# A vision tower on one core: routing tables written earlier, a new order at the experts' start, a decay-attention head on VectorE, and grouped last stores

## The reference

```python
h = _L0_tok_ref(x, ...)                              # patches, class token, positions
h = _layernorm(h + _L0_attn_ref(h, ...))             # 16 heads of 16, causal
h = _layernorm(h + _L0_ffn_ref(h, ...))              # int8 fake-quantised MLP
h = _layernorm(h + _L1_attn_ref(h, ...))             # decay attention
h = _layernorm(h + _L1_ffn_ref(h, ...))              # fixed-point MLP
h = _layernorm(h + _L2_attn_ref(h, ...))
h = _layernorm(h + _L2_ffn_ref(h, ...))              # 8 experts, top 2
h = _layernorm(h + _L3_attn_ref(h, ...))             # latent attention with rope
h = _layernorm(h + _L3_ffn_ref(h, ...))              # fake-quantised gated MLP
```

## Time and profile before

| what | us |
|---|---|
| three runs | 1116.05, 1113.37, 1104.77 |
| median | 1113.37 |
| the profiled execution | 1114.32 |
| its span, first to last instruction | 1112.5 |
| share of the span: PE 82%, PEld 61%, DVE 55%, ACT 47%, POOL 30% | |
| mean granted TensorE clock | 0.888 |

### The profile page before, as it was taken

The page is one execution under the profiler, slowest core; times in us unless marked ns, Lnnn a source line. Parts: engine busy times, 40 slices in busy tenths (PEclk is TensorE's granted clock), DMA queues, the critical chain, the costliest instruction groups (busy, mean ns, idle before and its releaser), DMA issues. The chain is left out here.

```text
span 1112.5 us, 26159 instructions
## 1 busy us (share of the span) xinstructions
PE 909.6 (82%) x10336; PEld 674.0 (61%) x10336; DVE 606.8 (55%) x1306; ACT 527.1 (47%) x940; POOL 335.2 (30%) x426
## 2 busy tenths in 40 slices
PE   4889958389999789958996299999478998989564
PEld 4878735267777557647885144444267777777332
DVE  3566746656666469764664524232655573542585
ACT  2354638366656379735452155554123333442354
POOL 1203320545544100021323315442254553432101
PEclk8999958699999979879997599999799998989775
DMA  5300020200000000001001963222320000000001
GB/s 181 118 3 2 3 105 15 80 1 2 1 0 1 12 35 0 1 4 47 3 3 54 392 225 73 40 47 41 73 81 3 2 3 2 3 3 1 1 1 44
DMA packets 23973, 47.40 MB, mean 43 GB/s; under 512 B 4386, under 2 KB 15640, under 8 KB 23221
## 3 DMA queue, kind: packets, MB, share of 16 engines
q1 hardware_dynamic: 19524, 39.09, 10.1%
q0 software_dynamic: 4336, 6.74, 3.3%
HBM read 38.35 MB, written 7.47 MB: 41 GB/s over the span
## 5 line engine op out<-in xcount | busy, mean ns | idle before, releaser
L2731 PE MATMUL psum<-L2f_EW,weights_even 128*64 x176 | 83.0, 616 | 2.9 <-ACT weights_even L2430 2.1
L2732 PE MATMUL psum<-L2f_W,weights_even 128*64 128x512 f32 x176 | 83.0, 616 | 0.0
L2391 POOL DMA_INDIRECT expert_sums<-weights_even,L2f_target x20 | 36.5, 1825 | 77.8 <-DVE weights_even L2613 68.4
L2626 DVE TENSOR_TENSOR weights_even<-psum,weights_even 128x512 f32<-128x512 f32 x22 | 15.2, 692 | 77.1 <-PE psum L2732 75.1
L1057 PE MATMUL psum<-L_cT,weights_odd 128*128 128x222 f32 (+1 forms) x192 | 45.2, 366 | 12.7 <-DVE L_by_sin L944 11.0
L2438 ACT ACTIVATE L2f_W<-L2f_EW 128x1024 f32 x44 | 46.3, 1053 | 15.4 <-DMA L2f_EW<-experts 8.2
L2247 PE MATMUL psum<-weights_even,L1f_H 128*111 128x256 f32 x176 | 47.3, 427 | 7.4 <-DVE L1f_H L2178 7.4
L2731 PEld LDWEIGHTS psum<-L2f_EW,weights_even 128*64 128x64 f32 x176 | 22.9, 140 | 46.6 <-issue 46.6
L419 ACT ACTIVATE L_PT<-psum 101x296 f32<-101x296 f32 x64 | 27.0, 421 | 48.2 <-PE psum L615 48.1
L876 ACT ACTIVATE L_U<-psum 128x592 f32<-128x592 f32 x32 | 21.2, 663 | 60.0 <-PE psum L1108 60.0
L2247 PEld LDWEIGHTS psum<-weights_even,L1f_H 128*111 128x111 f32 x176 | 35.1, 202 | 18.7 <-DVE L1f_H L2178 8.7
(11 more groups left out here) (459 smaller groups left out, 2627.2 us busy)
## 6 DMA issues: line engine op xcount, KB each, us to landing
L2f_EW<-experts SPq DMA_DIRECT2D x24, 512.0 KB, 7.4
weights_even<-L_w SPq DMA_DIRECT2D x4, 1024.0 KB
patch_ring<-patches SPq DMA_DIRECT2D x11, 333.0 KB
expert_sums<-L_blank SPq DMA_DIRECT2D x1, 1184.0 KB
out<-X SPq DMA_DIRECT2D x10, 111.0 KB
weights_odd<-L_wo SPq DMA_DIRECT2D x1, 1024.0 KB
expert_rows<-X SPq DMA_DIRECT2D x1, 960.0 KB
expert_sums<-X SPq DMA_DIRECT2D x1, 960.0 KB
```

Of the source, the lines that this page charges most:

```text
L2731: nc.tensor.matmul(core.bank(bank)[PAIR[0], :], xsT[:, j % 2, c, PAIR[0]], own, start=c == 0, stop=c == KD - 1)
L2732: mm = nc.tensor.matmul(core.bank(bank)[PAIR[1], :], xsT[:, j % 2, c, PAIR[1]], cols(W1[:, part], KD, NF)[:, c], start=c == 0, stop=c == K ...
```

## The change

Four edits stand in the diff.

1. Tables: the copies of X into `expert_rows` and `expert_sums` move from the experts' stage into the pair attention of the stage before. As soon as a unit of two tiles is normalised (units 0 to 4, so tiles 0 to 9), SP starts four transfers for it: 96 and 15 rows into each table. Only the last tile's 74 rows are still copied in the experts' stage, before and behind the weights. The two semaphores live in `Route` now.
2. Experts' order: on VectorE `source_and_target()` runs ahead of the owners, and on ScalarE `x_T(0)` runs ahead of the up copy.
3. Decay head: the first tile's statistics run ahead of the wait for the stage's weights, its normalising runs on VectorE (three instructions, semaphores `rstd_of_first` and `x_first`) with only the reciprocal standard deviation left on GpSimd, and the low parts of the weights are cut into one in front of the loop and three behind the low part of the first transposed tile.
4. Last stage: the final norm runs in groups of 4, 4, 2 and 1 tiles, the first three on ScalarE; the stores go out by group, each as 96 and 15 rows (the last as 64 and 10); and the first gate step waits for four transposed blocks, the second for all six.

```diff
@@ pair_attention, sync
+                    for u in range(NU - 1):
+                        sp.wait_ge(norm_done, u + 1)
+                        for table, sem in (("expert_rows", route.rows_out), ("expert_sums", route.sums_out)):
+                            by_row = core.dram[table][2 * u * R:2 * (u + 1) * R, :].rearrange("(t p) d -> p t d", p=R)
+                            for rows in (slice(0, 96), slice(96, R)):
+                                sp.dma_start(by_row[rows], X[rows, 2 * u:2 * (u + 1), :]).then_inc(sem, 16)
                     sp.wait_ge(blank_out, 16)
@@ decay_attention, gpsimd
-                    if live(i, 0):
+                    if isinstance(i, int) and i == 0:
+                        pool.wait_ge(pvar, 1)
+                        rstd_on_pool(core, prs[:R, 0], pmv[:R, 0, 1:2]).then_inc(rstd_of_first, 1)
+                    elif live(i, 0):
@@ decay_attention, vector
+                input_stats(0, 0)
                 dve.wait_ge(mine[0], mine[1])
                 for j in range(4):
                     nc.vector.tensor_copy(mask[:R, j, :], w["mask_tri"])
+                dve.wait_ge(rstd_of_first, 1)
+                nc.vector.tensor_scalar(xin[:R, 0], X[:R, 0, :], pmv[:R, 0, 0:1], prs[:R, 0], ALU.subtract, ALU.mult)
+                dve.drain()
+                nc.vector.tensor_tensor(xin[:R, 0], xin[:R, 0], w["L1_gamma"], ALU.mult)
+                dve.drain()
+                nc.vector.tensor_tensor(xin[:R, 0], xin[:R, 0], w["L1_beta"], ALU.add).then_inc(x_first, 1)
+                low_part(0)
                 nc.vector.tensor_copy(decay[:R], w["decay"]).then_inc(set_up, 1)
...
-                    if isinstance(i, int) and i == 0:
-                        for n_, c in enumerate("akqv"):
-                            dve.wait_ge(w_high, n_ + 1)
-                            nc.vector.tensor_tensor(W[1][:, n_], cols(w[f"L1_w{c}"], KD, DI), W[0][:, n_], ALU.subtract).then_inc(w_low, 1)
+                    if isinstance(i, int) and i == 1:
+                        for n_ in range(1, 4):
+                            low_part(n_)
@@ decay_attention, tensor
-                        pe.wait_ge(x_staged, f + 1)
+                        if isinstance(f, int) and f == 0:
+                            pe.wait_ge(x_first, 1)
+                        else:
+                            pe.wait_ge(x_staged, f)
@@ experts_ffn, sync
-                for p in SPLIT:
-                    sp.dma_start(by_tile(rows, p, 0, WHOLE), X[p, 0:WHOLE, :]).then_inc(rows_out, 16)
-                sp.dma_start(rows[WHOLE * R:B * T, :], X[AGAIN:R, WHOLE, :]).then_inc(rows_out, 16)
+                sp.dma_start(rows[WHOLE * R:B * T, :], X[AGAIN:R, WHOLE, :]).then_inc(route.rows_out, 16)
@@ experts_ffn, scalar
                 second_half(0, GATE, gate_1)
+                x_T(0)
                 act.wait_ge(ups_in, 16 * NEX)
                 second_half(0, UP, up_1)
-                x_T(0)
@@ experts_ffn, vector
                 V.scalar_tensor_tensor(counts, first, 1.0 / 64.0, blocks, ALU.mult, ALU.add)
+                source_and_target()
                 dve.drain()
@@ quantised_glu
+        ENDS = [(0, 4), (4, 4), (8, 2), (10, 1)]
+        ON_ACT = 3
-        tail = SplitNorm(core, st, sb)
+        tail = SplitNorm(core, st, sb, ENDS)
...
-                for t in range(NT):
-                    ...
+                for t0, k in ENDS[:ON_ACT]:
+                    sp.wait_ge(tail.act_norm, t0 + k)
+                    by_row = out[t0 * R:(t0 + k) * R, :].rearrange("(t p) d -> p t d", p=R)
+                    for rows in (slice(0, 96), slice(96, R)):
+                        sp.dma_start(by_row[rows], X[rows, t0:t0 + k, :]).then_inc(stored, 16)
+                sp.wait_ge(tail.dve_norm, 1)
+                for rows in (slice(skip, skip + 64), slice(skip + 64, R)):
+                    sp.dma_start(out[(NT - 1) * R + rows.start - skip:(NT - 1) * R + rows.stop - skip, :], X[rows, NT - 1, :]).then_inc(stored, 16)
...
-                pe.wait_ge(xt_done, NXB)
                 for n, (g, c) in enumerate(steps):
+                    if n < 2:
+                        pe.wait_ge(xt_done, 4 if n == 0 else NXB)
```

More of the change, by code:

```diff
@@ L1340, in _, with input_stats, low_part @@
             def _(dve):
+                def input_stats(i, p):
+                    nc.vector.bn_stats(pstat[:R, p], X[:R, i, :])
+                    dve.drain()
+                    nc.vector.bn_aggr(pmv[:R, p], pstat[:R, p]).then_inc(pvar, 1)
+                def low_part(n):
+                    dve.wait_ge(w_high, n + 1)
+                    nc.vector.tensor_tensor(W[1][:, n], cols(w[f"L1_w{'akqv'[n]}"], KD, DI), W[0][:, n], ALU.subtract).then_inc(w_low, 1)
+                input_stats(0, 0)
                 dve.wait_ge(mine[0], mine[1])
@@ L1354, in scores_out @@
                                                   core.bank(u)[:R, 0:4 * R]).then_inc(s_done, 1)
-                    if live(i, 0):
-                        after(dve, x_staged, i - 1)
-                        nc.vector.bn_stats(pstat[:R, p], X[:R, i, :])
-                        dve.drain()
-                        nc.vector.bn_aggr(pmv[:R, p], pstat[:R, p]).then_inc(pvar, 1)
+                    if live(i, 0) and not (isinstance(i, int) and i == 0):
+                        after(dve, x_staged, i - 2)
+                        input_stats(i, p)
                     if F:
@@ L2544, in _, with source_and_target @@
                                         inside_b[:R, u, p].unsqueeze(2).broadcast_to([R, k, 128]), ALU.is_equal).then_inc(placed, 1)
+                def source_and_target():
+                    dve.wait_ge(mark_ps, 1)
+                    found = core.bank(4)[:, 0:2 * NS]
+                    V.tensor_scalar(empty[:], found[:, 0:NS], ROUND, ROUND + 1.0, ALU.add, ALU.subtract)
+                    dve.drain()
+                    V.tensor_tensor(mark[:], empty[:], found[:, NS:2 * NS], ALU.add)
+                    dve.drain()
+                    V.tensor_scalar(source[:], mark[:], 0.0, None, ALU.max).then_inc(source_done, 1)
+                    V.tensor_scalar(empty[:], mark[:], 0.0, w["spare_row"], ALU.is_lt, ALU.mult)
+                    dve.drain()
+                    V.scalar_tensor_tensor(target[:], mark[:], w["own_sums"], empty[:], ALU.add, ALU.add).then_inc(target_done, 1)
                 V.scalar_tensor_tensor(counts, first, 1.0 / 64.0, blocks, ALU.mult, ALU.add)
+                source_and_target()
                 dve.drain()
@@ L2916, in _ @@
                         finish(t - 3)
-                tail.on_dve(dve, 2)
+                tail.on_dve(dve, 3)
             @block.scalar
@@ L2956, in _ @@
                 tail.on_act(act, 1)
+                tail.on_act(act, 2)
             @block.tensor
```

47 lines of the change are left out of this document (14 added, 33 removed).

## The result

The changed kernel took 1092.6 us (median of four runs, 1088.4 to 1096.4) beside 1109.2 for the kernel before: 16.6 us less by the medians. The ratio is 0.9845, with a 95% interval of 0.9802 to 0.9888, which is 17.2 us. A second measurement of the same pair gave 0.984 (0.9781 to 0.9899). The forecast was 14.6 us less. It started from a median of 1113.37 for the kernel before; a fourth run brought that median to 1109.2. The profiled execution has a span of 1086.6 us, 25.9 less than before. That is more than the change gave, as the lengths of the stages show. Each is taken from the first instruction of a stage to that of the next.

What follows compares the result with a forecast made beforehand. Stage heads and tails were taken as chains of waits, the experts' tiles as TensorE-bound, the end as transfers. Terms 4.6 + 0 + 3.0 + 0.7 + 6.3 = 14.6 us off 1113.37 gave 1098.8; range 1088 to 1107.

Steps and rivals of the forecast that it cites:

- Decay head, 4.6 forecast: Start of the decay attention: first projection starts 4.6 us earlier, bounds 3.3 to 4.95.
- The 3.3: Decay head's low bound: mask copies could slow GpSimd as the weight split did, leaving a term of 3.3 us.
- Tables, 0: Table transfers moved into the pair attention: cost 0 there, at most 1 us.
- the prediction's sign: Experts' start: after the change VectorE does not wait for the down weights.
- Experts' order, 3.0: Experts' start: first gate matmul comes 3.0 us earlier, bounds 1.5 to 4.0.
- The 22 tiles behind start earlier by as much: Experts' tiles: all start earlier by the head's 3.0 us, since TensorE fills them.
- Last stage, 0.7 + 6.3: Last stage: first gate step 0.7 us earlier; end of the last stores 6.3 us earlier, bounds 5.0 and 6.8.
- term 6.8: Final stores: by the skill page the last 64 KB land 2.15 us behind their start, making the gain 6.8 us.
- (b): Stores: the row split fails and few engines serve them; only 8.3 us come, time 1105; chance 0.08.
- (a): Experts gain nothing: the gather or gate product takes up what the weights give free; time 1102; chance 0.15.
- (d): Experts' tiles or decay head: broken-up starts keep TensorE's clock at 1.2 GHz; four such tiles give 1117; chance 0.05.
- case (c): More comes: weights flowing alone shorten gather and half clock, or upper bounds throughout; about 1095 to 1091; chance 0.10.

Runs made afterwards that it cites:

- e2: Changed kernel with both table copies put back in the experts' stage, ahead of and behind the weights: experts' stage 199.6 us, ratio to the kernel before 0.9906.
- e6: Changed kernel with only the first tile's normalising put back on GpSimd: first projection at 8.0 us, decay stage 176.2 us, second pair attention 108.3 us.
- e7: Changed kernel with only ScalarE's order put back, up copy ahead of the first tile's evacuation: first gate matmul at 30.7 us, experts' stage 196.8 us.
- e4: Changed kernel with stores by group but not cut by rows: 12.6 us from last norm to the end, ratio to the kernel before 0.9948.
- b1: Kernel before, with only the last stage's first gate step waiting for four transposed blocks: its first gate matmul at 8.4 us, experts' stage 203.9 us.
- e5: Changed kernel with only the weights' low parts put back in one piece ahead of the loop: first projection at 9.3 us, decay stage 179.2 us.

## Why the prediction was right, step by step

**Decay head, 4.6 forecast; 5.4 at the projection, 6.0 and 4.0 over the stage.** The path was as told, but the gain at the projection lies above the term's upper bound of 4.95. The masks were mis-sized: I let them end 1.9 behind the stage's start, and they ended 1.2 behind it, since the statistics cost nothing there. That gave nothing by itself, for VectorE then waited 0.78 for GpSimd's result. The 0.8 us came in small pieces: that result 0.2 sooner than taken (1.96 behind the start for 2.15), VectorE's split, sums copy and statistics 2.05 in place of 2.4, and the low part and the step to the projection 0.4 in place of 0.6. GpSimd's deviation took 0.9 as taken. The 3.3 in which the mask copies slow GpSimd did not come: only the first of its two steps ran beside them, in 0.24, and it was VectorE that waited, for the memset.

**Tables, 0.** Right for the transfers, by e2, e6 and the starts. The transfers cost the attention nothing. What they removed was worth more than the prediction says: it has VectorE's wait for the downs as a step with no price. One reading was too quick: at 411 GB/s the downs were to be in 33 to 34 us behind the stage's start, and they landed at 37.0, with the DMA at 381 GB/s over the first 30 us. So VectorE did wait for them, against the prediction's sign, but for less time than TensorE had left. e2 is 4.8 and 2.8 us of stage longer than the two executions of the changed kernel, and the experts were 5.0 and 3.0 shorter than before.

**Experts' order, 3.0; 3.1 and 2.5 at the first gate matmul.** Each step stood: gather, then gate product, which came last of the two, then transpose, evacuation, number. In the first execution two sizes were off and cancelled, which is luck: the product ended 28.9 us behind the stage's start (28.3 forecast) and the number's load was overlapped to 0.24. In the second the load took 0.81. Beside the early tables only VectorE's move carries it, ScalarE's nothing (e7). Over the stage it came to 5.0 and 3.0. The 5.0 are the 3.1, 0.6 that the second tile no longer lost to the number's load (0.22 for 0.81), and by my estimate 1.3 of the clock (half of 2.5), which rose 3.0 us behind the first gate matmul and not 5.6; in the second execution it rose at 5.8. "The 22 tiles behind start earlier by as much" was therefore only a floor in that one.

**Last stage, 0.7 + 6.3.** The first gate step gained 0.9 and the last norm came 0.4 earlier relative to the last matmul (0.7 and 0.4 forecast). The last bytes landed 2.4 us behind the last norm's end (1085.7 against 1083.38) and not 3.0: from that norm to the span's end it is 6.7 us less. The estimate by the Trainium skill's page DMA: Bandwidth & Descriptors, section Anatomy of one DMA (2.15 behind the start, term 6.8), was the better one, with 2.2 measured; I had leaned on the scatter's 4.0. The page gives its figure for transfers that GpSimd starts, and these were SyncE's.

**Rivals.** (b) is dead by e4, (a) by the first gate matmul. (d) did not come in the tiles (clock 1.00 from 625.85 on), but a clock that falls at a pause is real: it costs about 3 us in b1's experts and 1.5 in e2's (the rest of e2's loss is the wait itself). In the pair attention the changed kernel runs 3.4 us at half the clock, by my estimate 1.7 of the 2.2 it lost there.

**The sum.** The range held (1088 to 1107). The median of 1092.6 lies 6.2 below the forecast of 1098.8, in case (c), and most of that is not a larger gain: 4.2 of it are the base, which came out at 1109.2 and not 1113.37. The other 2.0 to 2.6 us are the gain above the 14.6, and that is within what the ratio's interval leaves open (12.4 to 22.0 us). The prediction's bounds also add up a little wrong: the terms give 16.45 at most and not 16.7, and 8.8 at least if the tables cost their 1.

## What to carry to other kernels

Compare stage by stage, not span by span: untouched stages differed here by up to 9 us between executions, while the heads that the change touched repeated within 0.1 (projection) to 1.1 us (first gate matmul). Cut a store's rows so that sixteen engines share them before grouping it; grouping alone made it worse here. A move of work onto another engine paid little here until what was queued there moved out of its way (0.5 us of projection in e5, 4.0 with both), and filling a time in which an engine is blocked anyway costs nothing.

## What was not expected

VectorE's mask copies wait for GpSimd's memset to end (they end 0.37 us behind it in both kernels). A late transfer costs more than its wait: 3.06 us of TensorE's idling were followed by 3.4 us at half the clock (e2). And the load of the expert's number held TensorE for very different times. Ahead of the second tile it took 0.81 and 2.13 us in the two executions of the kernel before and 0.21 to 0.27 in all twelve since. Ahead of the first it took 0.24 in six of those twelve and 0.81 to 0.92 in three. With the tables early and VectorE's order changed, the stage took 194.0 to 194.8 with the short load (five executions, the clock rising 31.9 to 33.1 us into the stage) and 196.8 to 196.9 with the long one (three, 36.4 to 36.5). Why the load differs is open: it was not tried apart.
